# Attention written out without loops: the max split on GpSimd, the turned parts copied by ScalarE, four banks for the first half head

## What is computed

```python
x = x + _L0_attn_a_ref(_layernorm(x), ...)      # selective scan
x = x + _L0_ffn_ref(_layernorm(x), ...)
x = x + _L0_attn_b_ref(_layernorm(x), Wq, bq, Wk, bk, Wv, bv, Wo, bo)
x = x + _L0_ffn_ref(_layernorm(x), ...)

# _L0_attn_b_ref, 16 heads of 16 channels, S = 4096
q, k, v = split_heads(x @ Wq + bq), split_heads(x @ Wk + bk), split_heads(x @ Wv + bv)
q, k = _rope(q), _rope(k)
scores = einsum('bhqd,bhkd->bhqk', q, k) / sqrt(16)
attn = einsum('bhqk,bhkd->bhqd', softmax(scores, axis=-1), v)
out = attn_by_tokens @ Wo + bo
```

## Time and profile before

| | us |
|---|---|
| median of 3 runs | 3761.28 |
| lowest, highest | 3759.84, 3768.51 |
| the profiled execution's own time | 3761.9 |
| its span, first to last instruction | 3760.2 |
| `attention`, first DMA to the last row maximum, in the span | 854.4 to 3538.1 |

### The profile page before, as it was taken

How to read it: one execution, slowest core, us unless ns; L and a number is a source line. 1 busy time by engine, 2 the same in 40 slices (tenths; PEclk the granted TensorE clock), 3 DMA queues, 4 the chain that set the end, 5 groups by cost and what they waited for, 6 DMA issues and landing times. The chain is left out here.

```text
span 3760.2 us, 77817 instructions
## 1 busy us (share of the span) xinstructions
PE 3472.7 (92%) x22853; PEld 1321.2 (35%) x22880; DVE 3393.0 (90%) x5278; ACT 2582.1 (69%) x4673; POOL 606.2 (16%) x436
## 2 busy tenths in 40 slices
PE   6688887885999999999999999999999999999988
PEld 3122222440233333333333333333333333333334
DVE  5899998785999999999999999999999999999616
ACT  5444443470488887888788788878878887878844
POOL 2689897071000000000000000000000000000020
PEclk9899999995799999999999999999999999999999
DMA  1000000152101001010101101010100101010011
GB/s 60 1 1 1 0 0 0 55 119 40 26 3 29 15 18 29 3 28 3 29 6 28 29 3 28 3 29 3 29 27 6 29 3 29 3 29 5 3 54 45
DMA packets 49398, 80.10 MB, mean 21 GB/s; under 512 B 12400, under 2 KB 39536, under 8 KB 44912
## 3 DMA queue, kind: packets, MB, share of 16 engines
q1 hardware_dynamic: 48496, 73.99, 8.3%
q10 hardware_dynamic: 512, 1.05, 0.2%
HBM read 53.37 MB, written 21.23 MB: 20 GB/s over the span
## 5 line engine op out<-in xcount | busy, mean ns | idle before, releaser
L1450 DVE TENSOR_REDUCE part_max<-max_scores 128x1 f32<-128x512 f32 x4096 | 2545.4, 684 | 111.1 <-PE max_scores L1260 45.0
L1423 ACT ACTIVATE prob<-scores 128x512 f32<-128x512 f32 x4096 | 2115.8, 603 | 621.6 <-PE scores L1296 619.3
L1296 PE MATMUL scores<-q_rows,k_rows 64*128 64x512 bf16 x4096 | 1283.5, 382 | 0.0
L1303 PE MATMUL scores<-q_rows,k_rows 35*128 35x512 bf16 x4096 | 1233.9, 380 | 0.0
L1340 PE MATMUL acc<-prob,v_ones 128*32 128x512 f32 x8192 | 1095.8, 607 | 0.0
L1260 PE MATMUL max_scores<-k_twin,q_twin 64*128 64x512 bf16 x2048 | 801.3, 391 | 56.3 <-DMA k_twin<-qk_parts 49.7
L1263 PE MATMUL max_scores<-k_rows,q_rows 64*128 64x512 bf16 x2048 | 801.9, 392 | 32.0 <-issue 18.8
L1263 PEld LDWEIGHTS max_scores<-k_rows,q_rows 64*128 64x128 bf16 x2048 | 189.8, 93 | 929.0 <-DVE part_max L1450 855.7
L1296 PEld LDWEIGHTS scores<-q_rows,k_rows 64*128 64x128 bf16 x4096 | 381.7, 93 | 294.4 <-PE scores L1303 24.0
L1303 PEld LDWEIGHTS scores<-q_rows,k_rows 35*128 35x128 bf16 x4096 | 378.3, 94 | 187.2 <-ACT prob L1423 38.8
L1192 POOL COPY v_ones<-v_all 128x512 f32 (+1 forms) x16 | 9.7, 609 | 2436.3 <-PE acc L1340 2436.2
(11 more groups left out here) (121 smaller groups left out, 1420.3 us busy)
## 6 DMA issues: line engine op xcount, KB each, us to landing
qk_parts<-roped_parts SPq DMA_DIRECT2D x64, 192.0 KB, 2.9
q_rows<-qk_parts SPq DMA_DIRECT2D x192, 64.0 KB
k_rows<-qk_parts SPq DMA_DIRECT2D x180, 64.0 KB
q_twin<-qk_parts SPq DMA_DIRECT2D x128, 64.0 KB
x_res<-in_x SPq DMA_DIRECT2D x4, 1024.0 KB, 9.0
rope_trig<-in_trig SPq DMA_DIRECT2D x4, 1024.0 KB, 9.3
att_t<-acc_sb SPq DMA_DIRECT2D x128, 32.0 KB
att_all<-att_t SPq DMA_DIRECT2D x8, 512.0 KB, 9.0
```

The lines of the kernel that those rows point to most:

```text
L1296: return nc.tensor.matmul(sc[:, n % SB, :], k_rows[0:LANE, par, kt * P:(kt + 1) * P], q_rows[0:LANE, par, q0:q0 + CH], start=(j == 1), sto ...
L1303: return nc.tensor.matmul(sc[:, n % SB, :], k_rows[LANE:KM, par, kt * P:(kt + 1) * P], q_rows[LANE:KM, par, q0:q0 + CH], start=(j != 1), s ...
L1423: nc.scalar.activation(prob[:, t % PBUF, j * CH:(j + 1) * CH], sc[:, n % SB, :], ACT.Exp, scale=SCALE).then_inc(exp_done, 1)
L1450: nc.vector.tensor_reduce(part_max[:, t, c:c + 1], mx[:, unit_bank(h, half, u), :], AXX, ALU.max).then_inc(dve_read, 1)
```

## The change

The feed-forward, scan and projection stages keep their code, but for one line of `attention_project`: in `qk_parts` the two halves of a row (s) now stand inside the channel (r) and not outside it. So 16 rows of a head and part are one dimension, and `load_rows` and `load_even_blocks` issue one DMA of 16 rows for each two of 8.

In `attention`:
- All 16 heads are written out on every engine; no loop and no register is left. The unused path over ScalarE and GpSimd is gone.
- Block 0: the four banks of the scores and the other four take turns as two groups (`wide_banks`). TensorE fills four banks with four units, VectorE reduces all four (128x2048) in one instruction to one column; 32 of these in place of 128.
- Head 0's loads are cut in two: what the products of block 0 need (16 DMAs, `first_loaded`), and the rest (`rest_loaded`), which is first waited for ahead of block 1.
- The split: VectorE keeps only the row maximum (`row_max`), and takes it one unit later, after unit 0 of the next block. The other four steps of the split are GpSimd's (`split_max`). `part_max` has two buffers.
- The turn stands ahead of unit 7 (TURN_AT = 7), which is i = 0 of step 29. The copy of the turned parts is ScalarE's (`copy_turned`), after the exponentials of step 29.

The diff, cut to this:

```diff
-TURN_AT = 6
+TURN_AT = 7
@@ attention_project
-  mem.qk_parts[a, :, s, h * HP:(h + 1) * HP, bass.ts(i, CH)].rearrange("s p t -> p s t"),
+  mem.qk_parts[a, :, h * HP:(h + 1) * HP, s, bass.ts(i, CH)].rearrange("s p t -> p s t"),
@@ attention
-        part_max = sb("part_max", [P, QT, NC + 2 * FOLD], F32)
+        part_max = sb("part_max", [P, 2, QT, NC], F32)
+        banks = ctx.enter_context(nc.psum_tensor("att_banks", [P, 8, CH], F32))
+        sc, acc, mx = banks[:, 0:SB, :], banks[:, SB, :], banks[:, SB + 1:SB + 1 + MB, :]
+        WIDE = 4
+        TURN_STEP = (MAXU + TURN_AT - LEAD) // 4
+        def wide_banks(g):
+            return banks[:, g % 2 * WIDE:(g % 2 + 1) * WIDE, :]
-                for s in range(2):
-                    r = base + n * DK + s * DK // 2
-                    eng.dma_start(rows[r:r + DK // 2, par, :],
-                                  mem.qk_parts[which, part, s, bass.ds(h * (DK // 2), DK // 2), :]
-                                  ).then_inc(rows_loaded, 16)
+                if n >= skip:
+                    r = base + n * DK
+                    eng.dma_start(rows[r:r + DK, h % 2, cols],
+                                  mem.qk_parts[which, part, h * (DK // 2):(h + 1) * (DK // 2), :, cols].rearrange(
+                                      "r s t -> (r s) t")).then_inc(done, 16)
-            with eng.Fori(0, (H - 2) // 2) as pair:
-                body(2 * pair + 1, 1, False, False)
-                body(2 * pair + 2, 0, False, False)
@@ sync
-                load_rows(sp, q_rows, 0, 0, Q_SLOTS, 0, 0)
-                load_rows(sp, q_twin, LANE, 0, Q_TWIN, 0, 0)
+                load_rows(sp, q_rows, 0, 0, Q_TWIN, 0, first_loaded, cols=now)
+                load_rows(sp, q_twin, LANE, 0, Q_TWIN, 0, first_loaded, cols=now)
+                load_rows(sp, q_rows, 0, 0, Q_TWIN, 0, rest_loaded, cols=then)
+                load_rows(sp, q_twin, LANE, 0, Q_TWIN, 0, rest_loaded, cols=then)
+                load_rows(sp, q_rows, 0, 0, Q_SLOTS, 0, rest_loaded, skip=len(Q_TWIN))
@@ gpsimd
+                def split_max(b):
+                    pool.wait_ge(low_ready, b + 1)
+                    if b >= 1:
+                        pool.wait_ge(turn_ready, b)
+                    nc.gpsimd.tensor_copy(neg_parts[:, 0, cols], neg_max[:]).then_inc(split_step, 1)
+                    ...
+                    nc.gpsimd.tensor_tensor(neg_parts[:, 2, cols], neg_rest[:], neg_parts[:, 1, cols],
+                                            ALU.subtract).then_inc(neg_ready, 1)
@@ tensor: bank_free, then block 0
+                    if q == TURN_AT:
+                        pe.wait_ge(max_copied, b)
+                for u in range(MAXU):
+                    g = u // WIDE
+                    if u % WIDE == 0 and g >= 2:
+                        pe.wait_ge(first_read, g - 1)
+                    max_product(wide_banks(g)[:, u % WIDE, :], 0, u // NC, u % NC).then_inc(first_ready, 1)
+                pe.wait_ge(rest_loaded, REST_LOAD)
+                pe.wait_ge(first_read, MAXU // WIDE)
@@ scalar: copy_turned, and its call in step
+                def copy_turned(b):
+                    if b > 0:
+                        act.wait_ge(max_moved, b * (16 * NPART))
+                    act.wait_ge(turn_ready, b + 1)
+                    nc.scalar.activation(max_rows[:], turned(), ACT.Copy).then_inc(max_copied, 1)
+                    if kt == TURN_STEP and b + 1 < 2 * H:
+                        copy_turned(b + 1)
@@ vector
-                    steps.link(nc.vector.tensor_copy(neg_parts[:, 0, cols], neg_max[:]))
-                    ...
-                    copy = nc.vector.tensor_copy(max_rows[:], turned(last))
+                for g in range(MAXU // WIDE):
+                    dve.wait_ge(first_ready, (g + 1) * WIDE)
+                    nc.vector.tensor_reduce(part_max[:, 0, t, m:m + 1], wide_banks(g), mybir.AxisListType.XY,
+                                            ALU.max).then_inc(first_read, 1)
+                row_max(0)
+                for b in range(1, 2 * H):
+                    max_units(b, 0 if b == 1 else 1, MAXU)
+                    if b + 1 < 2 * H:
+                        max_units(b + 1, 0, 1)
+                    row_max(b)
```

More of the change, by code:

```diff
@@ L1335, in weigh @@
                         pe.wait_ge(v_ready, h + 1)
-                    if kt == 0 and later(2 * h + half):
+                    if kt == 0 and 2 * h + half > 0:
                         pe.wait_ge(acc_read, 2 * h + half)
@@ L1385, in _ @@
+                for h in range(H):
+                    for t in range(STEPS):
+                        step(h, t)
+                weigh(H - 1, STEPS - 1)
             @block.scalar
             def _(act):
[L1387 to L1392 removed]
@@ L1394, in copy_max @@
-                def copy_max(h, half, u):
-                    own = sum(by_act(h, half, v) for v in range(u))
-                    act.wait_ge(even_ready if u % 2 == 0 else odd_ready, lane_ready(h, half, u))
-                    if not (is_first(h, half) and own < COPIES):
-                        act.wait_ge(pool_read, acts_done(h, half, u) - COPIES)
-                    nc.scalar.activation(max_copy[:, own % COPIES, :], mx[:, unit_bank(h, half, u), :],
-                                         ACT.Copy).then_inc(act_read, 1)
@@ L1443, in _, with max_units @@
+                load_rows(act, k_rows, 0, 1, K_TWIN, 0, first_loaded)
+                load_even_blocks(act, 0, first_loaded)
+                load_rows(act, k_rows, 0, 1, K_SLOTS, 0, rest_loaded, skip=len(K_TWIN))
+                copy_turned(0)
+                for h in range(H):
+                    for t in range(STEPS):
+                        step(h, t)
+                copy_block(2 * H - 1)
             @block.vector
             def _(dve):
-                def max_units(h, half, first, end):
+                def max_units(b, first, end):
```

476 lines of the change are left out of this document (175 added, 301 removed).

## The result

| | before | after |
|---|---|---|
| median of 4 runs, us | 3763.24 | 3640.78 |
| lowest, highest | 3759.84, 3768.51 | 3640.42, 3642.65 |
| span of the profiled execution | 3760.2 | 3639.0 |

The ratio is 0.9674, with a 95% interval of 0.9658 to 0.9691: faster by 3.3%. The profiled span fell by 121.2 us, where the sum of the terms said 114.4.

A forecast was written before the change was run, and what follows sets the result against it. The prediction took a step to be one ring through TensorE and VectorE, 2.49 us. Its terms, -51.5 - 37.0 - 6.1 - 19.8 = -114.4 us, gave 3646.9 us from a median of 3761.28, range 3626 to 3684 (8 in 10).

The forecast's parts named there:

- The ring: Attention step: product, reduce, handoff, product and weighing in turn through TensorE and VectorE, 2.49 us; VectorE alone needs 2.39.
- Loops out: Attention with all heads written out: 30 periods between row maxima at 81.25 us each, -51.5 us.
- Split and turn: Split on GpSimd and moved turn: a block pays 0.44 us for 1.65, in sum -37.0 us (-18 to -46).
- GpSimd's price: Split's four steps on GpSimd in each block: about 1.2 us, within 3.3 us available, no wait.
- ScalarE's copy: Copy of turned parts after step 29's exponentials: about 0.35 us, ending at 0.85, next exponentials due at 0.90.
- Block 0: 32 four-bank reduces at 2.19 us take 70.1 us for 76.6: -6.5 us, less 0.4 for the first reduce.
- First load: Head 0's load before the first product: 16-row DMAs, 1.25 MB needed; product at 868, not 887.83, -19.8 us.
- B: Rival: register instructions cost nothing, or other stalls fill in; only six round ends go. 3663 us, chance 0.13.
- C: Rival: the turn's handoffs eat what the split gave, TensorE stopping some 1.2 us. 3683 us, chance 0.12.
- F: Rival: gaps come as often in straight code, so the -51.5 us falls away. 3698 us, chance 0.05.
- D: Rival: steps get shorter, losing half of the 0.1 us over VectorE's own 2.39. 3599 us, chance 0.05.
- E: Rival: slower than before, GpSimd's split late at every turn; decides from 7.0 us, 3793 us at 8. Chance 0.02.

The follow-up runs named there:

- b_unroll: Kernel before with all 16 heads written out and nothing else changed: 3713.9 us, ratio 0.9882.
- b_two_rounds: Kernel before with its loop as two rounds of six heads, heads 13 and 14 written out, GpSimd keeping seven rounds: 3733.3 us, ratio 0.9933.
- a_split_dve: Kernel after with the split's four steps back on VectorE behind the row maximum: 3668.3 us, ratio 0.9755.
- a_turn6: Kernel after with the turn back ahead of unit 6, before the weighing of step 28 (TURN_AT = 6): 3662.2 us, ratio 0.9728.
- a_pool_4_more: Kernel after with four more chained casts of 128x16 on GpSimd ahead of each split: 3641.1 us, ratio 0.9672.
- a_copy_dve: Kernel after with the copy of the turned parts back on VectorE, ahead of unit 7's reduce: 3642.0 us, ratio 0.9687.
- a_dma8: Kernel after with the old qk_parts layout and twice as many DMAs of 8 rows, head 0's loads still cut in two: 3653.4 us, ratio 0.9717.
- a_half_reduce: Kernel after with each max reduce of blocks 1 to 31 over only the first 256 of 512 columns: 3593.1 us, ratio 0.9554.
- a_pool_16_more: Kernel after with 16 more chained casts of 128x16 on GpSimd ahead of each split: 3765.1 us, ratio 1.0005.

## Why the prediction was right

**The frame held.** The ring of 2.49 us a step is still there, and what the change takes away lies between the steps. The sum of 114.4 was 6.8 short of the profiled 121.2; 2.1 of that is the scatter ahead of the attention, and 4.4 the 30 periods. In its order:

- *Loops out, -51.5.* `b_unroll` measures 48.7 over the same 30 periods. Its periods are 81.35 in the mean and not 81.25, as one is 82.8 by a fall of the clock, and six are 81.4 for a reason that stays open. That the six round ends carry some 35 and register instructions the rest was right, by `b_two_rounds`.
- *Split and turn, -37.0.* From `b_unroll` to after, the 30 periods fall by 2440.4 - 2396.9 = 43.5, against 36.3 forecast. This is the term that was sized too small. What is left was put at 0.44 us a block, and is 0.30. The weighings around a split and turn in the kernel after start at 1100.41, 1103.00, 1105.68 and 1108.16: the step with the row maximum is 0.10 over 2.49, the one with the turn 0.19. The row maximum was put at 0.22. It takes 0.19 from start to start, where I had read 0.32 from before's trace, in which a dependent step stood behind it; less the slack of 0.1 that leaves the 0.10. The turn with its copy was put at 0.22, and is 0.19. And the 128 units fill 79.57 in the straight code, not 79.6. Besides, `b_unroll`'s period of 82.8 is gone, too. The prediction didn't say what brings the gain: by `a_split_dve` the four steps on GpSimd are worth 0.83 us a block, by `a_turn6` the place of the turn 0.57, together 1.40 beside the 1.35 found.
- *GpSimd's price, 1.2 us for four steps.* It is 1.05 (1100.90 to 1101.95): a step of 16 columns costs 0.20 or 0.22, near the row for one column, as the prediction took it. The way from the row maximum to the turn is 3.44 us. Even double the time is hidden, by `a_pool_4_more`.
- *ScalarE's copy.* It takes 0.27 us, not 0.35, and holds nobody up. That it left VectorE brought nothing by itself, though: by `a_copy_dve`, VectorE's hole behind the turn holds it.
- *Block 0, -6.1.* 5.8 by the traces; 2.20 us from start to start for a reduce over four banks ((70.42 - 2.28) / 31), as worked out from 1.04 ns a column.
- *First load, -19.8.* 20.2. The packets' reading was right: sixteen rows a DMA nearly halve the loading time (24.2 to 13.2 us). The Trainium skill ("DMA: Bandwidth & Descriptors", Why a DMA increments its semaphore by 16 and not by 1) says that a DMA is spread over the largest number of engines, up to 16, that divides its slowest dimensions; the 24.2 and 13.2 us, and the 50% of the engines' time in `a_dma8`, agree with that.
- *Not in the sum:* the stages ahead end 2.1 us earlier in the profiled execution. That is no gain of the change: with the same code ahead of it, the attention's first DMA starts anywhere from 852.3 to 854.8 us in the kernel after and the `a_` runs, and at 853.1 to 854.4 in `before`, `b_unroll` and `b_two_rounds`.

**The rivals.** B falls by `b_two_rounds`, C by the trace of the kernel after, in which the split is done 2.05 us ahead of the turn (and by `a_pool_4_more`), F by `b_unroll`, and D as a unit still takes 0.622. D took that half of the ring's 0.1 over VectorE's 2.39 could go; `a_half_reduce` shows that this half, 0.05, is all that a faster VectorE can give, as TensorE alone takes 2.44. E did not come, but its deciding point was too far out. The prediction put it at 7.0 us for GpSimd's four steps, by adding lateness alone. In `a_pool_16_more` they and their delay take from 2025.62 to 2030.85, 5.2 us, and the gain is gone, as a wait of 2.2 costs 1.6 more in the mean through the clock. The same is to be seen behind a round's end of before. TensorE's weighing there, then the window of that stretch:

```profile
2144.21 1.72 PE L1340 MATMUL acc<-prob,v_ones 128*32 128x512 f32 x8
```

```profile
2143.30:2145.30 2.00, 2.00 (x14) 0.38 (x10) 1.46 (x3) 1.78 (x4) 0.00 (x0) 0.50 0.50 156
```

So an idle of 3.75 us made a period 5.9 longer: it set the next product back by 3.8, and the step after it took 4.19 us (the products at 2141.67 and 2145.86) in place of 2.49, 1.7 more; the last 0.4 were not followed.

## What to carry to other kernels

Where two engines limit a loop in turn, price each side work by whether it stands in the ring: here 1.65 us of small steps a block became 0.30, some 0.83 by moving four of them to an engine that had 3.4 us for them, and some 0.57 by putting the turn behind the weighing. The copy that was moved as well was free either way, since it fitted in a hole. An idle of TensorE cost more than its length in 29 of the 30 waits looked at here, as the granted clock fell behind them, so give a handoff in such a loop slack, and count a late one at more than its lateness. And look at the packets of a short, urgent load before you count its bytes: twice the rows in a DMA nearly halved the time here.

## What the runs showed of the hardware that I had not expected

- After waits of 2.2 us on TensorE, at 30 turns of `a_pool_16_more`, the granted clock fell to 0.50 behind 29 and stayed at 1.00 behind one. In four cases it stayed low for about twice as long as in the other 25, which made the period 1.4 us longer. After the wait at 2031.00 it fell 1.7 us behind the wait's end, in other blocks right at the end. A wait of 3.75 in before did the like.
- Much smaller gaps brought it once, too: in one of 30 periods of `b_unroll` the clock fell to 0.50 at about 2598.9, behind TensorE's idles of 0.38 and 0.19 us, which the period before has too (at 2514.93 and 2517.32), without a fall.
- Of two chained VectorE reduces, the short one of 128x16 columns, 0.28 us long, moves the next by 0.19 only; four dependent steps of 0.17 behind it start 0.31 and then 0.21 us after each other, and move the reduce by 0.84 more.
- In the last block, making eight products in another order changed a step from 2.27 and 2.54 by turns to 2.64, at the same number of products and with the same exponentials.
